# The seam between two stages: when the first load is issued, and which blocks go first

## The reference

```python
t_eff = clip(t[0], 1e-8)
x_spec = einsum('nk,nc->kc', adj, x)                          # stage 1
coefs = exp(-evals * t_eff)[:, None]
x1 = layernorm(x + einsum('nk,kc->nc', adj, coefs * x_spec))  # stage 2
adj_hat = adj + eye(N)
y = (adj_hat / adj_hat.sum(1, keepdims=True)) @ (x1 @ W) + b  # graph convolution
return layernorm(x1 + tanh(y))
```

## Time and profile before

| what | us |
|---|---|
| median of three runs | 632.07 |
| lowest and highest | 630.26, 633.38 |
| the profiled execution | 631.55 |
| its span in the trace | 628.4 |
| TensorE busy in the span | 583.3 (93%) |
| VectorE, ScalarE, GpSimd busy | 514.9, 396.7, 365.1 |
| core's granted TensorE clock, mean | 0.986 |

### The profile page before, as it was taken

How to read it: one execution, slowest core, us unless ns; L and a number is a source line. 1 busy time by engine, 2 the same in 40 slices (tenths; PEclk the granted TensorE clock), 3 DMA queues, 4 the chain that set the end, 5 groups by cost and what they waited for, 6 DMA issues and landing times.

```text
span 628.4 us, 7998 instructions
## 1 busy us (share of the span) xinstructions
PE 583.3 (93%) x2450; PEld 445.6 (71%) x2450; DVE 514.9 (82%) x604; ACT 396.7 (63%) x859; POOL 365.1 (58%) x206
## 2 busy tenths in 40 slices
PE   2999999999996689999999999999999969999992
PEld 2887788778774456667888888888888746656561
DVE  3889989989887999797979789697776586999992
ACT  4999999999986735645665656445444445545552
POOL 0000000000131888878999999779787879896961
PEclk9999999999999699999999999999999999999997
DMA  8999999999999999999996999387985399999101
GB/s 270 389 387 386 387 387 387 387 387 387 387 337 322 276 307 257 293 272 255 307 264 167 269 265 310 96 225 212 263 240 165 83 338 329 348 334 329 47 17 50
DMA packets 141288, 174.66 MB, mean 278 GB/s; under 512 B 6852, under 2 KB 105412, under 8 KB 141256
## 3 DMA queue, kind: packets, MB, share of 16 engines
q1 hardware_dynamic: 88976, 121.68, 61.2%
q10 hardware_dynamic: 52280, 52.58, 30.7%
HBM read 172.13 MB, written 2.11 MB: 277 GB/s over the span
## 4 chain that ended last, share of the span: by engine, by line
PE 64%; DMA 10%; POOL 8%; DVE 7%; ACT 4%; issue 3%; SPq 2%; ACTq 1%; POOLq 0%; DVEq 0%
PE ps L748 13%; PE ps L750 13%; PE ps L749 13%; DMA raw<-in_adj_dram 10%; POOL lo L404 7%; PE ps L744 6%; PE ps L724 5%; PE ps L725 5%; PE ps L726 5%; DVE vt L588 3%; ACT hi L437 2%; PE ps L813 1%; PE ps L816 1%; ACTq L322 1%; SPq L336 1%
## 5 line engine op out<-in xcount | busy, mean ns | idle before, releaser
L404 POOL TENSOR_TENSOR lo<-vt,hi 128x1024 fp32r<-128x1024 f32 x129 | 327.4, 2566 | 56.4 <-ACT hi L452 55.4
L588 DVE STREAM_TRANSPOSE vt<-raw 128x1024 f32<-128x1024 f32 x184 | 222.3, 1227 | 63.2 <-PE ps L750 52.6
L452 ACT ACTIVATE hi<-vt 128x1024 fp32r<-128x1024 f32 x163 | 169.8, 1061 | 111.8 <-DVE vt L588 94.1
L571 DVE TENSOR_TENSOR lo<-raw,hi 128x1024 fp32r<-128x1024 f32 x124 | 153.5, 1240 | 22.2 <-ACT hi L437 21.9
L437 ACT ACTIVATE hi<-raw 128x512 fp32r<-128x512 f32 x256 | 158.2, 621 | 15.1 <-DMA raw<-in_adj_dram 5.4
L386 POOL TENSOR_TENSOR lo<-raw,hi 128x1024 fp32r<-128x1024 f32 x4 | 10.7, 2682 | 180.7 <-ACT hi L437 180.7
L724 PE MATMUL ps<-hi,xg_hi 128*128 128x512 f32 x256 | 102.8, 401 | 8.4 <-DVE lo L571 7.2
L748 PE MATMUL ps<-hi,s_hi 128*128 128x512 f32 x232 | 99.2, 428 | 9.5 <-issue 5.2
L725 PE MATMUL ps<-lo,xg_hi 128*128 128x512 f32 x256 | 100.7, 393 | 0.0
L726 PE MATMUL ps<-hi,xg_lo 128*128 128x512 f32 x256 | 100.4, 392 | 0.0
L748 PE MATMUL ps<-hi,p_hi 128*128 128x512 f32 x206 | 88.3, 429 | 6.8 <-POOL lo L404 6.8
(11 more groups left out here) (64 smaller groups left out, 499.2 us busy)
## 6 DMA issues: line engine op xcount, KB each, us to landing
raw<-in_adj_dram SPq DMA_DIRECT2D x64, 1024.0 KB, 14.2
raw<-in_adj_dram SPq DMA_DIRECT2D x88, 512.0 KB, 9.7
raw<-in_adj_dram ACTq DMA_DIRECT2D x88, 512.0 KB, 11.7
late_raw<-in_adj_dram SPq DMA_DIRECT2D x8, 512.0 KB, 11.6
late_raw<-in_adj_dram ACTq DMA_DIRECT2D x8, 512.0 KB, 13.5
xn<-in_x_dram SPq DMA_DIRECT2D x8, 256.0 KB, 12.3
x_sb<-in_x_dram SPq DMA_DIRECT2D x8, 256.0 KB, 13.9
out_dram<-x_sb ACTq DMA_DIRECT2D x8, 256.0 KB, 2.9
```

The lines of the kernel that those rows point to most:

```text
L404: nc.gpsimd.tensor_tensor(lo[:, slot(p), :], vt[:, slot(p), :], hi[:, slot(p), :].bitcast(f32), ALU.subtract).then_inc(pool_lo_ready, 1)
L452: nc.scalar.activation(hi[:, slot(s), :], vt[:, slot(s), :], ACT.Copy).then_inc(hi_ready, 1)
L571: nc.vector.tensor_tensor(lo[:, q % RING1, :], raw[:, k, 2 * h:2 * h + 2, :].rearrange("p r n -> p (r n)"), hi[:, q % RING1, :].bitcast(f3 ...
L588: nc.vector.transpose(vt[:, slot(s), :].rearrange("p (m a i) -> p m a i", m=2, a=RB), load_buffer(st.load).rearrange("p (a m e i) -> p e m ...
```

## The change

Three edits around the seam; the work itself stays the same but for one new semaphore.

- ScalarE issues its half of load 0 behind chunk 6 and `s_hi` of unit 2 instead of behind chunk 3, its half of load 1 behind `s_hi` of unit 3, that of load 2 behind `hi` 0, and that of load 3 behind `s_hi` of unit 4.
- Turn 0 and `hi` 0 come ahead of units 4 to 7: VectorE's row is turn 0, copy 6, turn 1, copy 7, turn 2, `s_lo` 4, turn 3, `s_lo` 5. TensorE multiplies steps 0 and 1 ahead of the turn of the last pair.
- `s_hi` and `s_lo` of units 6 and 7 go into the loop over p, at p = 2 and 3; `full` of units 4 to 7 goes to p = 4 to 7, behind `s_lo`, and a whole step of the spectral product waits for it on TensorE (`full_ready`).

SyncE's and GpSimd's lists are unchanged.

```diff
             with act.Fori(0, (NG - 2) // 2) as d:
                 visit1(2 * d + 1, 1, d + 2)
                 visit1(2 * d + 2, 0, d + 2)
-            for i in range(NK + 4):
-                if i < NK:
-                    chunk1(LAST, i)
-                if i >= 3 and i % 2 == 1 and i // 2 - 1 < NU:
-                    wait_buffer(act, i // 2 - 1)
-                    load_quarters(act, i // 2 - 1, (2, 3))
-                if 0 <= (k := i - 4) < NK:
-                    act.wait_ge(sT_done, k // 2 + 1)
-                    ...
-                    if k >= WHOLE_FROM:
-                        for jj in (2, 3):
-                            last = nc.scalar.activation(full[:, k - WHOLE_FROM, (jj - 2) * C:(jj - 1) * C],
-                            ...
-                    last.then_inc(shi_ready, 1)
-                if i >= NK + 2:
-                    hi_step(i - NK - 2)
+            def spectrum_hi(k):
+                act.wait_ge(sT_done, k // 2 + 1)
+                ...
+                last.then_inc(shi_ready, 1)
+
+            def spectrum_full(k):
+                act.wait_ge(s_ready, k + 1)
+                for jj in (2, 3):
+                    ...
+                last.then_inc(full_ready, 1)
+
+            def first_load(n):
+                wait_buffer(act, n)
+                load_quarters(act, n, (2, 3))
+
+            act.wait_ge(coef_ready, 1)
+            for k in range(NK):
+                chunk1(LAST, k)
+                if k >= 4:
+                    spectrum_hi(k - 4)
+                if k == NK - 2:
+                    first_load(0)
+            first_load(1)
+            hi_step(0)
+            first_load(2)
+            hi_step(1)
+            spectrum_hi(4)
+            first_load(3)
+            spectrum_hi(5)
...
             for p in range(AHEAD, POSITIONS):
                 if p < STEPS:
                     hi_step(p)
+                if 6 <= p + 4 < NK:
+                    spectrum_hi(p + 4)
+                if WHOLE_FROM <= p < NK:
+                    spectrum_full(p)
...
-            for i in range(NK + 4):
+            for k in range(NK):
                 for h in range(2):
-                    if i < NK and 2 * i + h in LATE_DVE:
-                        half1(LAST, i, h)
+                    if 2 * k + h in LATE_DVE:
+                        half1(LAST, k, h)
-                if 0 <= (k := i - 2) < NK:
-                    ...
-                if 0 <= (k := i - 4) < NK:
-                    ...
-                if i >= NK + 1:
-                    turn_step(i - NK - 1)
+                if k >= 2:
+                    spectrum_out(k - 2)
+                if k >= 4:
+                    spectrum_lo(k - 4)
+            turn_step(0)
+            spectrum_out(6)
+            turn_step(1)
+            spectrum_out(7)
+            turn_step(2)
+            spectrum_lo(4)
             turn_step(3)
+            spectrum_lo(5)
...
                 if p + AHEAD < STEPS:
                     turn_step(p + AHEAD)
+                if 6 <= p + 4 < NK:
+                    spectrum_lo(p + 4)
                 if p < STEPS and not whole(p) and on_vector(p):
                     lo_step(p)
...
                 if whole(s):
                     pe.wait_ge(vturned, s + 1)
+                    if st.spectral:
+                        pe.wait_ge(full_ready, st.unit - WHOLE_FROM + 1)
...
                 chunk1(LAST, k, 1, False, True)
                 if k >= 3 and k % 2 == 1:
                     spectrum(k // 2 - 1)
-
+            products(0)
+            products(1)
             spectrum(NU - 1)
...
-            for p in range(AHEAD, POSITIONS):
-                if 0 <= p - LAG < STEPS:
+            for p in range(LAG + 2, POSITIONS):
+                if p - LAG < STEPS:
                     products(p - LAG)
```

More of the change, by code:

```diff
@@ L276, in spectral_then_graph_conv @@
         hi1_ready, lo1_ready, pool_lo1_ready, mm1_done = map(sem, ("hi1_ready", "lo1_ready", "pool_lo1_ready", "mm1_done"))
-        spec_out, sT_done, shi_ready, s_ready = map(sem, ("spec_out", "sT_done", "shi_ready", "s_ready"))
+        spec_out, sT_done, shi_ready, s_ready, full_ready = map(
+            sem, ("spec_out", "sT_done", "shi_ready", "s_ready", "full_ready"))
         vturned, hi_ready, lo_ready, pool_lo_ready, mm_done = map(
@@ L465, in _ @@
                 visit1(2 * d + 2, 0, d + 2)
-            for i in range(NK + 4):
-                if i < NK:
-                    chunk1(LAST, i)
-                if i >= 3 and i % 2 == 1 and i // 2 - 1 < NU:
-                    wait_buffer(act, i // 2 - 1)
-                    load_quarters(act, i // 2 - 1, (2, 3))
-                if 0 <= (k := i - 4) < NK:
-                    act.wait_ge(sT_done, k // 2 + 1)
[L474 to L479, removed]
-                    if k >= WHOLE_FROM:
-                        for jj in (2, 3):
-                            last = nc.scalar.activation(full[:, k - WHOLE_FROM, (jj - 2) * C:(jj - 1) * C],
-                                                        ps[:, k, jj * C:(jj + 1) * C], ACT.Copy,
-                                                        scale=coef[:, k, jj:jj + 1])
-                    last.then_inc(shi_ready, 1)
-                if i >= NK + 2:
-                    hi_step(i - NK - 2)
@@ new lines, in spectrum_hi @@
+            def spectrum_hi(k):
+                act.wait_ge(sT_done, k // 2 + 1)
+                for jj in range(JB):
+                    j = k * JB + jj
+                    last = nc.scalar.activation(s_hi[:, j * C:(j + 1) * C], ps[:, k, jj * C:(jj + 1) * C],
+                                                ACT.Copy, scale=coef[:, k, jj:jj + 1])
+                last.then_inc(shi_ready, 1)
+            def spectrum_full(k):
+                act.wait_ge(s_ready, k + 1)
+                for jj in (2, 3):
+                    last = nc.scalar.activation(full[:, k - WHOLE_FROM, (jj - 2) * C:(jj - 1) * C],
+                                                ps[:, k, jj * C:(jj + 1) * C], ACT.Copy, scale=coef[:, k, jj:jj + 1])
+                last.then_inc(full_ready, 1)
@@ L605, in _ @@
                 visit1(2 * d + 2, 0)
-            for i in range(NK + 4):
-                for h in range(2):
-                    if i < NK and 2 * i + h in LATE_DVE:
-                        half1(LAST, i, h)
-                if 0 <= (k := i - 2) < NK:
[L611 to L621, removed]
-                if 0 <= (k := i - 4) < NK:
[L623 to L630, removed]
-                if i >= NK + 1:
-                    turn_step(i - NK - 1)
@@ new lines, in spectrum_out @@
+            def spectrum_out(k):
+                dve.wait_ge(mm1_done, PAIRS * LAST + 2 * k + 2)
+                u = k // 2
+                if u >= 2:
+                    dve.wait_ge(sT_done, u - 1)
+                for e in range(2):
+                    last = nc.vector.tensor_copy(
+                        spec[:, u % 2, e * CW:(e + 1) * CW].rearrange("c (m q i) -> c q m i", m=JB, q=QN)
+                        [:, 2 * (k % 2):2 * (k % 2) + 2],
+                        ps[:, k, :].rearrange("c (q m e i) -> c e q m i", q=2, m=JB, e=2)[:, e])
+                last.then_inc(spec_out, 1)
@@ new lines, in spectrum_lo @@
+            def spectrum_lo(k):
+                dve.wait_ge(shi_ready, k + 1)
+                for jj in range(JB):
+                    j = k * JB + jj
+                    last = nc.vector.scalar_tensor_tensor(
+                        out=s_lo[:, j * C:(j + 1) * C], in0=ps[:, k, jj * C:(jj + 1) * C],
+                        scalar=coef[:, k, jj:jj + 1], in1=s_hi[:, j * C:(j + 1) * C].bitcast(f32),
+                        op0=ALU.mult, op1=ALU.subtract)
+                last.then_inc(s_ready, 1)
```

## The result

The changed kernel takes **642.69 us** (median of four, 640.58 to 643.04) against 631.51 for the kernel before in the same runs: ratio 1.0168, with an interval of 1.0133 to 1.0203, so 11 us slower. The profiled execution took 643.04, its span is 639.5 (before: 628.4). The forecast was 635.3 with a range of 631.8 to 639.0: the direction was right, the size was not. Of the 11.1 us in the span, 3.2 were foreseen and 7.9 were not.

The account below looks back on a forecast made before the run. The start of step 6's product, with TensorE as pace behind it, was taken as the bound; starting 3.2 us later, it took the profiled 631.55 to 634.8, on the median 635.3 us, range 631.8 to 639.0.

Parts of the forecast that it names:

- What bounds the kernel: Start of step 6's product sets the end, with TensorE as pace behind it, give or take about 1 us.
- Part 1, the issue: ScalarE's late half of load 0 is issued at about 191.1, some 14 us later than before.
- Part 1, the flight: Load 0 lands whole 11.2 us after ScalarE's issue, at 202.3 (199.9 to 204.9).
- Part 1, the last chunk: Stage 1's last chunk lands near 186.1 without ScalarE's half beside it; stage 1 ends only 0.4 us earlier.
- Part 2: Turn 0 comes first, at 202.3, 1.1 us earlier; the product of step 0 starts at L + 4.8.
- L: The moment load 0 has landed whole, from which the seam's later times are counted; forecast 202.3.
- Part 3: Last spectrum pair behind two products: `hi` 4 at L + 15.5, GpSimd idles 5.7 us, step 6 3.2 us later.
- Part 4: Moved `full` activations, `s_lo` 6 and 7, and ScalarE's later issues of loads 1 to 3 cost nothing.
- Late landing with the clock down again: Rival: L = 204.9 gives 5.8 us, TensorE's lower clock 2.6 more; 637.9 to 640.5 us; chance 0.18.
- the sum: Profiled execution 631.55 + 3.2 = 634.8 us; on the median 635.3 us.
- Stage 1's tail follows its loads: Rival: landing of chunks 5 to 7 sets stage 1's tail, 6.3 us earlier; 629.0 us; chance 0.10.
- The early landing: Rival: load 0 lands at 199.9, step 6 from 0.4 early to 0.8 late; 631.7 to 632.9 us; chance 0.22.

Follow-up runs that it names:

- the kernel with the pair ahead: Last follow-up: the changed kernel, loads still late, with TensorE turning the last spectrum pair ahead of the products of steps 0 and 1; 640.49 us, ratio 1.015.
- the one with load 1 held: The changed kernel, but SyncE issues its quarters of load 1 and all later loads only once load 0 has landed whole; 634.26 us (one execution).
- order with early loads: The changed kernel with ScalarE's loads 0 to 2 issued behind chunks 3, 5, 7 and load 3 right behind the last chunk; 630.68 us, ratio 0.9991.
- last chunk first: The changed kernel, but SyncE issues its half of load 0 only when the last chunk of stage 1 has landed; 638.06 us (one execution).
- order with early loads and degrees later: As order with early loads, with SyncE writing the degrees behind load 15 and reading them back behind load 19; 631.12 us, ratio 0.9995.
- load 4 by SyncE: The changed kernel, but SyncE issues all four quarters of load 4 and ScalarE none; 642.9 us, ratio 1.0189.

## Why the prediction was right or wrong, point by point

**What bounds the kernel: held.** Step 6 starts 10.5 us later, the span ends 11.1 later. It holds only up to load 8, which the prediction did not see: a lead at the seam of 3.7 us came to nothing there until the degrees' write was moved.

**Part 1, the issue: held.** Forecast 191.1, measured 191.73. Of these 0.6 nothing belongs to the change: with the same lists on ScalarE up to there, the kernel with the pair ahead issues at 190.56 and the one with load 1 held at 190.86.

**Part 1, the flight: this step failed.** Forecast 11.2 from the first issue, measured 14.5 (14.4 in the last kernel). The step took the row of loads at a quiet time, because "SyncE's half of load 0 has landed by then but its later loads share the engines". Both halves of that reason were wrong. SyncE's half of load 0 landed only at 196.9, 5 us behind ScalarE's issue. And its later loads did not share until about 198; ScalarE's quarters stood behind them. The rate was lower too: in 184 to 198, nearly all on SyncE's queue, the changed kernel moved 179 GB/s, and from 202 on 346 with both.

```profile
184.00:198.00 14.00, 12.31 (x56) 9.37 (x55) 12.10 (x27) 11.69 (x40) 3.77 (x2) 1.00 1.12 179
198.00:202.00 4.00, 1.33 (x10) 0.96 (x9) 0.24 (x1) 0.00 (x0) 0.00 (x0) 1.00 1.11 245
202.00:206.00 4.00, 0.00 (x0) 0.00 (x0) 0.00 (x0) 0.00 (x0) 0.00 (x0) 0.73 1.10 346
```

(Windows of the changed kernel: busy time of PE, PEld, DVE, ACT, POOL, then granted clock, DMA share, GB/s.) The kernel before moved 272 to 351 GB/s in the windows between 176 and 200, some of which stand in the earlier trace rows, while its ScalarE queue was fed. So moving half of a load later took rate from the seam for 14 us, and at 192 SyncE's loads, issued ahead, were still in the air. With load 1 held the flight is 9.3, near the 8.8 that the prediction had as its lower bound: the size was right for a pair that flies alone, and what it flew behind was left out. By the rule of the Trainium skill that the prediction weighed ("SBUF — State Buffer", section "Can I just issue two DMAs to hit both halves?"), load 0 would land at 204.8 by my estimate, nearer than my 202.3. But 346 GB/s from 202 to 206, with both queues, is again no 6% gain over one (200 GB/s from 191.7 to 197 on SyncE's alone, and 211 on ScalarE's alone from 194 to 200 with load 1 held); the rule came near for another reason.

**Part 1, the last chunk: failed, without a price.** It was to land at 186.1 and landed at 191.9, because SyncE's half of load 0 lies on it too. Stage 1 ended as said, TensorE's turns setting it.

**Part 2: held, counted from L.** The product of step 0 starts at L + 4.8, as forecast (211.02). It begins at granted 0.50 (211.02 to 213.75), 1.2 of 2.4 GHz, after 11.69 us without work on TensorE, but from 213.75 on the matmuls are short again: step 1 runs for the most part at the upper level (granted 0.90 from 213.75 to 215.30), and the turn of the last pair ends at L + 10.1 instead of L + 11.1.

**Part 3: the mechanism held, a term was missing.** GpSimd idles between its third and fourth `lo`, ended by ScalarE, 7.22 us where 5.7 was forecast; the three `lo` after it take 8.15 where 8.2 was forecast. `hi` 4 is ready at L + 17.5 instead of L + 15.5. Of these 2.0 us, the wait on an issue makes 3.2 and the earlier pair and shorter hand-overs take back 1.2. Without such an issue it is ready at L + 14.3 (order with early loads, where GpSimd goes on at 212.18) and GpSimd idles 4.72; in two more kernels without one (last chunk first; order with early loads and degrees later) it is L + 15.3 and L + 15.6, and GpSimd idles 5.72 and 6.10. So the forecast's sizes fit where no issue stands.

**Part 4: "costs nothing" was wrong for ScalarE's issues.** The part weighed when loads 2 and 3 would land and never how long their issue would hold ScalarE, and it did not list load 4, whose issue follows `hi` 3: in the new order `s_hi` 7 and `hi` 4, which GpSimd waits for, stand right behind it. ScalarE's list:

```profile
216.44 0.32 ACTq L323 DMA_DIRECT2D raw<-in_adj_dram  x1
...
216.79 4.81 ACTq L323 DMA_DIRECT2D raw<-in_adj_dram  x1
...
221.65 1.14 ACT L471 ACTIVATE s_hi<-ps,coef 128x128 fp32r<-128x128 f32 x4 [3.20 <-issue]
```

The activations up to 218.45 run on, and then `s_hi` 7 stands 3.20 us behind an issue of 4.81. In the earlier trace rows the issues of the same form take 0.88 for two and 0.32. Loads 1, 2 and 3 landed at 213.65, 223.02 and 229.92, 5 to 6 us later than this part had them, and still cost no turn a wait. That `full` costs nothing held: TensorE's whole products at 237.37, 240.48 and 243.58 follow without a wait.

**The rivals.** Late landing with the clock down again is the one that came, and further out than I had put it: L = 206.2 instead of 204.9, and after 8.99 us without work TensorE enters step 3 at granted 0.51:

```profile
227.20:231.20 4.00, 3.91 (x9) 3.12 (x10) 4.00 (x5) 2.77 (x6) 3.92 (x2) 0.51 0.71 152
231.20:236.00 4.80, 4.80 (x22) 3.94 (x21) 4.73 (x7) 2.27 (x4) 4.17 (x3) 1.00 0.96 269
```

GpSimd's `lo` 6 is done at 231.96, and step 6 starts at 233.29: TensorE, not GpSimd, is last by 1.3 us (2.6 was forecast for this). In the order with early loads it is the same 1.3, from 220.34 to 221.6, so L + 23.8 there agrees with my L + 23.7 by luck: two errors cancel, as `hi` 4 comes 1.2 earlier and TensorE is 1.3 late. With the degrees later they don't, and it is L + 25.9. What the sum left out is TensorE's own way to step 6: `lo` 3 on VectorE behind `s_lo` 7, and then steps 3 to 5 that begin at the lower clock. "Stage 1's tail follows its loads" falls, by the chunk that landed at 186.9 and did not move the end of stage 1. The early landing would have needed SyncE's load 1 out of the way.

**The sum, mended:** 3.2 forecast, + 0.6 issue, + 3.3 flight, + 2.0 `hi` 4, + 1.35 clock, + 0.6 behind step 6 = 11.05; measured 11.1 in the span. Shown by runs of their own are the flight (5 us of it, with load 1 held) and the issue that stands (2.8 from L to step 6, with load 4 by SyncE). The table bears the second out: of the kernels with the new order and late loads, three in which an issue of 3.9 to 4.8 us stands ahead of `s_hi` 7 need 27.1 to 27.6 us from L to step 6, two without need 24.3 and 25.3, and the one with load 1 held, where `s_hi` 7 stands only 0.71 us, 25.8. The 1.35 for the clock and the 0.6 behind step 6 are only read from the rows.

## What to carry to other kernels

When a transfer is moved later, ask first what is already queued at that moment: its flight then is not that of a load at a quiet time, and the same move can leave the transfers issued ahead on one queue, at a lower rate, until then. A DMA issue is an instruction of its engine, with a duration: count it on the path wherever a compute engine issues beside work that others wait for. And a lead won at one place has to be followed to the next bound: here the better order paid only once a 16 KB write was out of the way of a load.

## What the runs showed of the hardware that was not expected

At the seam a DMA issue of 512 KB mostly lasts 0.3 to 0.5 us on ScalarE, but some last 2.3 to 4.8 us, a few others 1 to 2, and the activations of that engine then stand too (3.20, 4.67 and 5.49 us in three kernels). Each of those of 2.3 us and more came when about three quarters or more (1.5 MB) were issued on ScalarE's queue and not yet moved, counted from its packets: 3.0 quarters ahead of the 3.79 us issued at 193.47 in the changed kernel, 3.3 ahead of the 4.81 us. Quarters that are merely not landed are no sign: in the kernel before, an issue at 192.84 took 0.51 us with five of them not landed, of which all but 2.3 quarters' bytes had moved. This is read from the traces; no run was made for it.

One queue feeding one half of the partitions moved 200 GB/s (SyncE's) or 211 (ScalarE's), both together 346. A queue as such can do more: in stage 1 SyncE's alone moved 387 GB/s (60 to 140 us), with chunks over all 128 partitions in packets of about 2 KB, where the quarters' are 1 KB. Whether the partitions or the packets make the difference for one queue no run tells apart.

And a write of 16 KB in 1024 packets needed 20.0 us to land, and the two quarters issued behind it 19.0 and 19.2, the second issued 7.8 us late; without it the same two took 12.9 and 17.5.
